# Normalising both feed-forwards' tokens inside their first group of products

## What is computed

```python
x = x + L0_attn(layernorm(x))   # gated delta rule, 6 heads of 64
x = x + L0_ffn(layernorm(x))    # F0: gelu(x Wg) * (x Wu) Wd, 4096 hidden, weights packed as 4-bit codes
x = x + L1_attn(layernorm(x))   # latent attention, 16 heads
x = x + L1_ffn(layernorm(x))    # F1: silu(x Wg) * (x Wu), 2 of every 4 kept by size, Wd, 2048 hidden

def _layernorm(x, axis=-1, eps=1e-05):
    m = jnp.mean(x, axis=axis, keepdims=True)
    v = jnp.var(x, axis=axis, keepdims=True)
    return (x - m) / jnp.sqrt(v + eps)
```

## Time and profile before

| | us |
|---|---|
| median of 3 runs (3054.35 to 3056.11) | 3055.91 |
| the profiled execution | 3056.75 |
| its span, first to last instruction | 3055.0 |
| TensorE busy | 2822.7 (92%) |
| VectorE busy | 1703.7 (56%) |
| ScalarE busy | 1075.3 (35%) |
| GpSimd busy | 787.4 (26%) |
| mean granted clock of TensorE, share of full speed | 0.955 |

### The profile page before, as it was taken

How to read it: one execution, slowest core, us unless ns; L and a number is a source line. 1 busy time by engine, 2 the same in 40 slices (tenths; PEclk the granted TensorE clock), 3 DMA queues, 4 the chain that set the end, 5 groups by cost and what they waited for, 6 DMA issues and landing times. The chain is left out here.

```text
span 3055.0 us, 37788 instructions
## 1 busy us (share of the span) xinstructions
PE 2822.7 (92%) x13750; PEld 2333.7 (76%) x13750; DVE 1703.7 (56%) x2571; ACT 1075.3 (35%) x1615; POOL 787.4 (26%) x830
## 2 busy tenths in 40 slices
PE   7966988679999999999999689999999869999998
PEld 7846878568888888888888558888888658888887
DVE  6855676464444544444553666666666354655554
ACT  3433433131111121112111357777777522222221
POOL 0038767100000000000000147777778500000000
PEclk9968988889999999999999879999999979999999
DMA  2243222110000010000000121111110010001001
GB/s 84 103 114 69 56 70 46 45 41 22 21 21 21 21 41 21 21 21 21 21 21 0 40 63 43 43 43 41 38 36 22 14 52 17 28 14 41 14 14 42
DMA packets 96407, 114.75 MB, mean 38 GB/s; under 512 B 47072, under 2 KB 73696, under 8 KB 94624
## 3 DMA queue, kind: packets, MB, share of 16 engines
q1 hardware_dynamic: 96288, 113.20, 12.5%
HBM read 86.16 MB, written 26.74 MB: 37 GB/s over the span
## 5 line engine op out<-in xcount | busy, mean ns | idle before, releaser
L1958 POOL TENSOR_TENSOR att_p_lo<-att_probs,att_p_hi 128x768 fp32r<-128x768 f32 x256 | 467.1, 1836 | 149.2 <-ACT att_p_hi L2015 147.8
L2111 DVE TENSOR_REDUCE att_top<-att_q_scores 128x1 f32<-128x1024 f32 x250 | 305.7, 1223 | 221.7 <-PE att_q_scores L2218 188.2
L297 DVE TENSOR_TENSOR fp_hidden<-fp_gelu,fp_up 128x512 f32<-128x512 f32 x128 | 88.1, 688 | 448.9 <-PE fp_up L75 386.1
L2026 ACT ACTIVATE att_probs<-att_k_scores 128x1024 f32<-128x1024 f32 x256 | 262.8, 1027 | 163.3 <-PE att_k_scores L2236 162.0
L1692 POOL MEMSET lat_power<- 128x16 f32 x1 | 0.1, 111 | 1079.0 <-POOLq L52 1079.0
L286 DVE TENSOR_TENSOR k_stream<-k_stream,fp_down 128x512 f32<-128x512 f32 x256 | 175.7, 686 | 90.8 <-PE fp_down L75 87.4
L347 ACT ACTIVATE fp_gelu<-fp_gate 128x512 f32<-128x512 f32 x128 | 76.3, 596 | 423.1 <-PE fp_gate L75 422.1
L73 PE MATMUL fp_gate<-f_feat_hi,fp_w_hi 128*128 128x512 f32 x512 | 200.3, 391 | 13.3 <-DVE fp_w_lo L266 13.3
L2015 ACT CAST att_p_hi<-att_probs 128x768 fp32r<-128x768 f32 x256 | 211.8, 828 | 0.0
L2218 PE MATMUL att_q_scores<-att_k_stack,att_q_stack 128*128 128x512 f32 x500 | 187.6, 457 | 13.8 <-DMA att_q_stack<-att_k_stack 10.3
L74 PE MATMUL fp_gate<-f_feat_lo,fp_w_hi 128*128 128x512 f32 x512 | 200.1, 391 | 0.0
(11 more groups left out here) (351 smaller groups left out, 6525.6 us busy)
## 6 DMA issues: line engine op xcount, KB each, us to landing
f_words<-codes SPq DMA_DIRECT2D x16, 768.0 KB
f_scale<-scales SPq DMA_DIRECT2D x16, 768.0 KB
f_staged<-w_sparse SPq DMA_DIRECT2D x12, 1024.0 KB, 4.9
qkv<-pf_rows SPq DMA_DIRECT2D x18, 512.0 KB, 2.8
dr_raw<-qkv SPq DMA_DIRECT2D x16, 576.0 KB, 6.2
att_q_stack<-rotated SPq DMA_DIRECT2D x128, 64.0 KB, 2.6
att_k_stack<-rotated SPq DMA_DIRECT2D x128, 64.0 KB, 2.6
k_stream<-hidden SPq DMA_DIRECT2D x4, 1024.0 KB, 10.2
```

The lines of the kernel that those rows point to most:

```text
L1958: pool.tensor_tensor(p_lo[:, buffer, :], probs[:, slot, 0:SPLIT], p_hi[:, buffer, :].bitcast(F32), ALU.subtract).then_inc(lo_done, 1)
L2026: act.activation(probs[:, t, :], k_scores[:], ACT.Exp).then_inc(exp_done, 1)
L2111: dve.tensor_reduce(top[buffer][:, STACK + t:STACK + t + 1], scores[:], AX.XY, ALU.max, negate=True).then_inc(max_done, 1)
```

## The change

The stage `normalise` is gone. The statistics of each tile are taken in the stage in front, soon after the tile has got its last addition: in the delta rule two tiles per chunk (`token_stats`), in the output projection two per pair (`stats`). Mean and variance are made in two parts: of tiles 0 to 3 early, in the stage in front (`token_moments` with EARLY, the same seven small instructions on four columns), and of tiles 4 to 15 at the start of the feed-forward (REST_TILES), with the power of each part on GpSimd (`inverse_deviation`).

In F0 the first codes and scales are loaded by SP in the delta rule, behind the residual rows of chunk 6, into a buffer that the rule's inputs had used; VectorE unpacks them in the last chunk (`first_codes`), into the buffer of `a_t`. In F1 the first gate and up weights are loaded and split in the output projection. Its staging buffers, `hidden`, `size` and the normalised tiles now lie in the space of the attention's `values`.

The feed-forward scales and turns only block 0 before its first products. The tiles of block tb + 1 are turned by PE in the middle of `gate_up` of block tb (after c = 0 of 2 in F0, after r = 1 of 4 in F1), into the accumulators of `down`; for that `down` of blocks 0 and 1 waits until the low features of the blocks two further are made. ScalarE and VectorE make high and low features there. The first group is written out on every engine, outside the loop over groups.

```diff
+def inverse_deviation(pool, norm, rows, group):
+    pool.wait_ge(norm.moments, 7 * group + 7)
+    pool.tensor_tensor(norm.rstd[:, rows], norm.var[:, rows], norm.power[:, rows], ALU.pow).then_inc(norm.rstd_done, 1)
+EARLY, REST_TILES = slice(0, SUB), slice(SUB, TILES)
...
+            def scale(i):
+                if i >= SUB:
+                    dve.wait_ge(turned_done, i - SUB + 1)
+                dve.tensor_scalar(normed[:, i % SUB, :], stream[:, i, :], norm.mean[:, i:i + 1],
+                                  norm.rstd[:, i:i + 1], ALU.subtract, ALU.mult).then_inc(normed_done, 1)
+            def low(i):
+                dve.wait_ge(hi_done, i + 1)
+                cols = slice(i * P, (i + 1) * P)
+                dve.tensor_tensor(feat_lo[:, :, cols], turned[i % SUB], feat_hi[:, :, cols].bitcast(F32),
+                                  ALU.subtract).then_inc(lo_done, 1)
...
+                    turning = first and t + 1 < BLOCKS
                     for c in range(2):
                         chunk = 2 * n + c
+                        if turning and c == 1:
+                            for i in tiles_of(t + 1):
+                                low(i)
...
+                    if first and t + 2 < BLOCKS:
+                        for i in tiles_of(t + 2):
+                            scale(i)
...
-            for nibble in range(2):
-                prepare(0, nibble)
+            dve.wait_ge(norm.rstd_done, 1)
+            for i in tiles_of(0):
+                scale(i)
             for nibble in range(2):
                 low_weights(dve, 0, 0, nibble)
+            for i in tiles_of(0):
+                low(i)
+            token_moments(dve, norm, REST_TILES, TILES, 1)
+            dve.wait_ge(norm.rstd_done, 2)
+            for i in tiles_of(1):
+                scale(i)
             body(0, True, False)
...
+                        if first and c == 0 and t + 1 < BLOCKS:
+                            for i in range(SUB * (t + 1), SUB * (t + 2)):
+                                high(i)
...
+            def turn(tb):
+                for j in range(SUB):
+                    i = SUB * tb + j
+                    if tb in (1, 2):
+                        pe.wait_ge(lo_done, i - SUB + 1)
+                    if tb == 3:
+                        pe.wait_ge(added, SUB + j + 1)
+                    pe.wait_ge(normed_done, i + 1)
+                    for kt in range(KT):
+                        last = pe.transpose(turned[j][:, kt, :], normed[:, j, feature_tiles_nibbles(kt)], ident[:])
+                    last.then_inc(turned_done, 1)
+            def gate_up(n, group, b, tb, first):
                 pe.wait_ge(w_hi_done, 2 * group + 4)
                 pe.wait_ge(w_lo_done, 2 * group + 4)
+                if first:
+                    pe.wait_ge(lo_done, SUB * (tb + 1))
...
+                    if first and c == 0 and tb + 1 < BLOCKS:
+                        turn(tb + 1)
+            def down(n, b, t, first):
+                if first and t < 2:
+                    pe.wait_ge(lo_done, SUB * (t + 3))
...
+            turn(0)
+            gate_up(0, 0, 0, 0, True)
+            body(0, True, False)
+            with pe.Fori(1, LOOPS - 1) as it:
+                body(it, False, False)
+            body(LOOPS - 1, False, True)
...
+            sp.wait_ge(qk_ps, FOURS * CHUNKS)
+            load_codes(sp, fp4, codes, scales, 0)
             load_residual(CHUNKS - 1)
...
+            def token_stats(c):
+                dve.wait_ge(written, 2 * c + 2)
+                for b in range(BATCH):
+                    tile = b * CHUNKS + c
+                    dve.bn_stats(token_norm.raw[:, tile, :], stream[:, tile, :]).then_inc(token_norm.stats_done, 1)
+            def first_codes(nibble, ops):
+                at = 3 * nibble
+                if 0 in ops:
+                    if nibble:
+                        dve.wait_ge(fp4.step, 3)
+                    else:
+                        dve.wait_ge(fp4.loaded, 32)
+                        dve.wait_ge(m_ps, FOURS * CHUNKS)
+                        dve.wait_ge(l_out, 16 * QUARTERS * CHUNKS)
+                    fp4.shift(dve, nibble).then_inc(fp4.step, 1)
+                if 1 in ops:
+                    dve.wait_ge(fp4.step, at + 1)
+                    fp4.mask(dve).then_inc(fp4.step, 1)
+                if 2 in ops:
+                    dve.wait_ge(fp4.step, at + 2)
+                    fp4.scaled(dve, nibble).then_inc(fp4.step, 1)
...
+                if c == CHUNKS - 1:
+                    first_codes(0, (0, 1, 2))
                 if c:
                     add_output(c - 1, 0)
+                if c >= 2:
+                    token_stats(c - 2)
+                if c == CHUNKS - 2:
+                    token_moments(dve, token_norm, EARLY, 2 * (c - 1), 0)
                 if ahead:
                     key_blocks(ahead)
                     query_blocks(ahead)
                 if c:
                     add_output(c - 1, 1)
                 corrected_values(c)
+                if c == CHUNKS - 1:
+                    first_codes(1, (0, 1))
                 gate_output(c)
                 decay_state(c)
                 add_state(c)
...
             output_sums(CHUNKS - 1)
             normalise_output(CHUNKS - 1)
+            first_codes(1, (2,))
             low_output(CHUNKS - 1)
+            token_stats(CHUNKS - 2)
             for b in range(BATCH):
                 add_output(CHUNKS - 1, b)
+            token_stats(CHUNKS - 1)
...
+            for part in range(2):
+                sp.dma_start(first[part][:], weights[0, part]).then_inc(arrived[part], 16)
...
+                if i in (6, 8):
+                    part = (i - 6) // 2
+                    act.wait_ge(arrived[part], 16)
+                    act.copy(w_hi[part][:], first[part][:]).then_inc(w_hi_done, 1)
...
+            def stats(i):
+                dve.wait_ge(added, i + 3)
+                dve.bn_stats(norm.raw[:, i, :], stream[:, i, :]).then_inc(norm.stats_done, 1)
+            def low_weights(part):
+                dve.wait_ge(w_hi_done, part + 1)
+                dve.tensor_tensor(w_lo[part][:], first[part][:], w_hi[part][:].bitcast(F32),
+                                  ALU.subtract).then_inc(w_lo_done, 1)
+            for i in range(2):
+                low(i)
+            for i in range(0, TILES, 2):
+                for ahead in (i + 2, i + 3):
+                    if ahead < TILES:
+                        low(ahead)
+                for tile in (i, i + 1):
+                    add(tile)
+                if i:
+                    for tile in (i - 2, i - 1):
+                        stats(tile)
+                if i == 6:
+                    token_moments(dve, norm, EARLY, SUB, 0)
+                if i in (8, 10):
+                    low_weights((i - 8) // 2)
+            for tile in (TILES - 2, TILES - 1):
+                stats(tile)
...
+                if g == 0:
+                    sp.wait_ge(turned_done, TILES)
...
+                    next_tiles = range(SUB * (tb + 1), SUB * (tb + 2)) if first and tb + 1 < BLOCKS else ()
+                    if first and tb == 0:
+                        dve.wait_ge(norm.rstd_done, 2)
+                    for i in next_tiles:
+                        scale(i)
                     for r in range(4):
+                        if r == 2:
+                            for i in next_tiles:
+                                low(i)
...
-            low_weights(0, 0)
-            low_weights(0, 1)
+            dve.wait_ge(norm.rstd_done, 1)
+            for i in range(SUB):
+                scale(i)
+            token_moments(dve, norm, REST_TILES, TILES, 1)
+            for i in range(SUB):
+                low(i)
             body(0, True, False)
...
+                        if first and r == 1 and tb + 1 < BLOCKS:
+                            for i in range(SUB * (tb + 1), SUB * (tb + 2)):
+                                high(i)
...
+                    if first and r == 1 and tb + 1 < BLOCKS:
+                        turn(tb + 1)
+            def down(n, g, tb, first):
                 if tb == 0:
                     pe.wait_ge(w_lo_done, 3 * g + 3)
+                if first and tb < 2:
+                    pe.wait_ge(lo_done, SUB * (tb + 3))
```

More of the change, by code:

```diff
@@ L452, in project_front @@
         padded = s.sb("padded", [P, 3, BATCH, CONV - 1 + SEQ])
-        rows = [s.sb(f"rows{q}", [P, BATCH, SEQ]) for q in range(3)]
+        homes = (fp4.weight[:].rearrange("p n c -> p (n c)"), fp4.early[:], fp4.early[:, BATCH * SEQ:])
+        rows = [home[:, 0:BATCH * SEQ].rearrange("p (b t) -> p b t", b=BATCH) for home in homes]
         turned = [s.ps(f"turned{b}", [P, KT, P]) for b in range(2)]
@@ L2359, in low, with add @@
                                   ALU.subtract).then_inc(lo_done, 1)
-            def add(i, b):
+            def add(i):
                 dve.wait_ge(out_done, i + 5)
-                tile = stream[:, bass.ds(i, 1), :]
```

(32 more changed lines are left out.)

398 lines of the change are left out of this document (191 added, 207 removed).

## The result

The changed kernel takes **3020.5 us** (median of four runs, 3017.5 to 3021.5) against 3055.1 for the kernel before, run beside it (3048.4 to 3056.1): ratio 0.988, 95% interval 0.987 to 0.989. It is faster by 35 us; forecast were 50, and 3020.5 lies outside the range of 2999 to 3013. The profiled execution took 3021.52 us, 1.8 more than its span.

What follows compares the result with a forecast made beforehand. TensorE, busy 92% of the span, was taken as the bound, with time to gain only where it stands still: 3056.75 - 26.6 (F0) - 23.9 (F1) - 0.8 = 3005.5 us, clock net 0; 8-in-10 range 2999 to 3013.

Steps and rivals of the forecast that it cites:

- Step (1): Last chunk of the delta rule: VectorE waits for the codes and unpacks them, so `dr_x_m` starts later, +2.2 us.
- The clock paragraph: PE's clock at the starts of F0 and F1 and in turn 2's wait: net 0, bounds -5 and +5 us.
- Rival A: Codes land later still and in-order VectorE stands in the last chunk, 4 to 8 us more: about 3012; chance 10%.
- Step (2): Statistics in the delta rule's earlier chunks, hidden behind VectorE's wait for PE: 0, upper bound 7 us.
- Step (3): Start of F0: first product at 609.4 instead of 641.47, -32.1 us.
- Steps (4) and (5): F0: three turns of 16 blocks inside the group, +4.7 us; `down(0)` waits for block 2's low features, +0.75 us.
- Steps (6) and (7): Output projection makes F1's first weights at no cost, 0; F1's first product at 2484.6 instead of 2516.24, -31.6 us.
- Step (8): F1's first group: turns 1 and 3 cost +3.2 us; turn 2 waits for VectorE's scales, +4.5 us.
- B: Block 0's selection lets PE go at once, `down(0)` does not wait, clock full at both starts: 2998 us; chance 10%.
- C: The statistics are not hidden and slow the chunk chain, and the projection's load is slowed: 3016 us; chance 6%.
- D: Turns between products hold the clock at 1.2 GHz through both first groups, slower than before: 3178 us; chance 2%.
- E: F0's first product still waits for codes and weights as before, only F1 gains: 3032 us; chance 2%.

Runs made afterwards that it cites:

- experiment 3: Changed kernel with the first group's codes and scales issued from SyncE some 38 us earlier; 3016.4 us.
- experiment 5: Changed kernel with 24 unread 128x128 products on PE ahead of its wait for the last chunk's `dr_x_m`; 3019.9 us.
- experiment 6: Changed kernel with 13 unread 128x128 products on PE ahead of its wait for the last chunk's `dr_x_m`; 3020.3 us.
- experiment 1: Changed kernel with 320 unused bytes per partition behind the norm's tensors of F1, which moves its features; 3012.9 us.
- experiment 7: Changed kernel with 64 unused bytes per partition behind the norm's tensors of F1; 3008.3 us.
- experiment 8: Changed kernel with 192 unused bytes per partition behind the norm's tensors of F1; 3018.1 us.
- experiment 4: Changed kernel with F1's scales of tiles 8 to 11 and 12 to 15 put ahead of VectorE's selection of blocks 0 and 1; 3016.2 us.

## Why the prediction was wrong, step by step

The step that failed most is one that the sum does not name: the price of a product in F1, put at no change. Its size is told below, behind the steps that have a number.

**Step (1)**, +2.2: measured +3.4 for `dr_x_m`, and +6.4 for the end of the stage. Two things failed. The codes came later: VectorE began at 570.59 in an execution whose anchor comes 0.87 us early, so 1.5 us behind the forecast of 570.0. From the issue of the codes to that start passed 12.3 us, where the step had 10.5. (In the six traces of this program `dr_x_m` came 2.0 to 3.8 us later than before, so +2.2 lies within what one execution can show; the tail behind it took 3.0 to 4.4 more in all six.) And the step stopped at `dr_x_m` and took everything behind it as unchanged. The clock paragraph looked only at the starts of F0 and F1. The wait that step (1) itself made, 3.57 us on PE, halved the clock for the thin products of the tail, +3.0 (experiments 3, 5 and 6). Rival A named the in-order VectorE at this place and priced it from 4 us on; it was right as a mechanism, its 4 us more did not come for `dr_x_m` (1.2 more), and it had the clock missing too.

**Step (2)**, 0: right. The anchor of chunk 6 came 0.9 us earlier, not later, with ten statistics ahead of it; its place varies by more than that from run to run (554.4 to 562.2 in these traces). **Step (3)**, -34.3 counted from the last addition: -34.2.

**Steps (4) and (5)**, +5.5: +6.2 up to the latent stage, and the nearness is in part luck. A turn of 16 blocks costs 1.9 us in F0 and not 1.58 (product starts at 621.03 and 623.10 around the first, the next step 0.08 longer), so 5.8 for three and not 4.7. And `down(0)` does not wait: its first product starts at 641.65, 0.37 us behind the last `fp_up`, so +0.1 and not +0.75. The clock at F0's start is as before: slow products from 612.83 to 618.94, 6.1 us (6.4 before), then fast ones.

**Steps (6) and (7)**, -31.6: -31.2. The projection became 0.2 us longer, less than its traces differ among each other, and F1 starts 9.44 us behind the last addition's start instead of 41.26.

**Step (8)**, +7.7: +8.2 once the places are mended (experiment 1). Turn 2's wait was 4.08 us where the step had 4.4. At F1's start 7 products are slow and not 12, 1.0 us gained; turn 2 at half clock takes 1.5. Net 0 for the clock was near enough in F1.

**What no step had**: +10.2 us in F1. The sum took every product to cost what it did before, because its instruction was the same. The diff moves the weights in front of the norm's 704 bytes and the features behind them; that is in the listing of the tensors, and I read it for its size only. 704 is not a multiple of 256. In F0 the same 704 bytes stand ahead of both operands, and nothing happened. The forecast needed this one check of the addresses. Had the products kept their rate, the time would have been about 3010 (3005.5 and the 4.2 of step (1)), within the range; experiments 1 and 7, where they did, measured 3012.9 and 3008.3.

**Rivals.** Of B's three parts one came, `down(0)` not waiting; the selection did not let PE go at once, and no start found the full clock from its first product. C did not come: no statistics showed. D did not come: products between turns stay fast. E did not come. The miss lay outside all five, in the rate of the products, where none of them looked. Of the signs named for being wrong, one came, less than 40 us gained; the codes landed before 572, and neither first group had other idle PE.

## What to carry to other kernels

When a change moves tensors, compare the places of the two operands of each long run of products in the old and the new layout, and compare the duration of one product in the two traces before looking for waits. Price a new wait on TensorE with what runs behind it at half clock, also in the middle of a stage: here 3.6 us of standing cost 3.0 more. A transfer that an in-order engine will wait for belongs in its queue when its buffer comes free (at 521, PE's last read was at 502), not where the program's text has it.

## What the runs showed of the hardware

- A 128x512 fp32r product takes 0.227 us from start to start if the stationary and the moving operand lie at equal places modulo 256 bytes of a partition, and 0.232 to 0.2335 us if the moving one lies 96, 128 or 192 further on, modulo 256. That is 3% of a product, and 2% of F1 (10.2 of 557 us) and of F0 (21.1 of 1082), whose down products are not touched. With 64 it was 0.229, and the three products of a triple differed, though their operands lie alike. Why this is so, and what other distances and types cost, no run here shows. The absolute place was not found to matter: products are fast with both operands at 0 (output projection, experiment 8), at 64 (F0) and at 128 (F1 before).
- TensorE's granted clock fell from 1.00 to 0.50 behind one wait of 3.57 us, and stayed at 1.00 when unread products filled it.
- Sixteen turns of 128x128 take 1.9 us at a granted clock of 1.00 (experiment 4 at 2493.76) and 3.7 at 0.50 (the changed kernel at 2457.39).
